# Two transformer layers on one core: a second transposed-x and shift tile, x in a ring of four, and new tables of jobs

## The reference

```python
xn = _layernorm(x)
x = x + _L0_attn_ref(xn, ...) + _L0_ffn_ref(xn, ...)   # differential attention: 2 x 16 maps of 4 features; FP6-quantised 128x128 product
xn = _layernorm(x)
x = x + _L1_attn_ref(xn, ...) + _L1_ffn_ref(xn, ...)   # rotary attention: 16 heads of 8 features; three products with +-1 weights
```

## Time and profile before

| | |
|---|---|
| median of 3 runs | 860.66 us |
| the profiled execution's own time | 859.55 us |
| its span, first to last instruction | 857.8 us |
| first exponential starts | 20.53 us |
| PE / ACT / DVE busy | 93% / 89% / 64% of the span |
| ACT's exponentials, 768 of them | 725.8 us busy |
| mean granted clock of TensorE | 0.989 |

### The profile page before, as it was taken

One profiled execution on the slowest core, in us unless ns is written; L12 is line 12 of the kernel. 1 busy time (PEld: TensorE's weight loads), 2 busy tenths in 40 slices (PEclk: granted clock), 3 DMA queues, 4 the chain that ended last, 5 costly groups with the idle time before them and its releaser, 6 DMA issues.

```text
span 857.8 us, 17781 instructions
## 1 busy us (share of the span) xinstructions
PE 801.4 (93%) x6735; PEld 283.6 (33%) x6735; DVE 551.5 (64%) x1216; ACT 764.2 (89%) x856; POOL 35.4 (4%) x56
## 2 busy tenths in 40 slices
...
GB/s 110 166 119 123 53 91 135 124 57 50 164 50 148 7 106 108 107 97 2 164 50 141 64 1 213 50 126 30 51 164 89 115 2 151 53 2 139 75 13 13
DMA packets 42114, 75.52 MB, mean 88 GB/s; under 512 B 5920, under 2 KB 7584, under 8 KB 42016
## 3 DMA queue, kind: packets, MB, share of 16 engines
...
...
## 4 chain that ended last, share of the span: by engine, by line
PE 70%; ACT 12%; DVE 9%; issue 5%; DMA 2%; SPq 1%; DVEq 0%; ACTq 0%
PE ps_pv L899 30%; PE ps_s L880 20%; ACT probs L726 12%; PE ps_misc L747 7%; PE ps_misc L751 7%; PE ps_misc L752 5%; PE ps_misc L740 2%; DMA q_ab<-shift 1%; DMA parts_dram<-qk_parts 1%; DVE pv_sb L1346 1%; DVE v_aug L1205 0%; DVE h_lo L1139 0%; ACT ff_out L676 0%; SPq L457 0%; DVE h_hi L1137 0%
## 5 line engine op out<-in xcount | busy, mean ns | idle before, releaser
L726 ACT ACTIVATE probs<-ps_s 128x1024 f32<-128x1024 f32 x768 | 725.8, 1048 | 54.8 <-PE ps_s L880 53.7
L899 PE MATMUL ps_pv<-probs,v_aug 128*32 128x512 f32 x3072 | 412.0, 608 | 8.6 <-ACT probs L726 4.6
L880 PE MATMUL ps_s<-q_ab,k_ab 18*128 18x512 f32 (+1 forms) x1088 | 142.6, 497 | 29.9 <-ACT probs L726 23.9
L880 PEld LDWEIGHTS ps_s<-q_ab,k_ab 18*128 18x128 f32 (+1 forms) x1088 | 54.6, 183 | 204.1 <-ACT probs L726 164.1
L899 PEld LDWEIGHTS ps_pv<-probs,v_aug 128*32 128x32 f32 x3072 | 61.7, 108 | 116.2 <-issue 82.8
L751 PE MATMUL ps_misc<-h_hi,k_w 128*128 128x512 f32 x192 | 85.8, 447 | 2.4 <-DVE v_aug L1205 1.2
L880 PE MATMUL ps_s<-q_c,k_c 34*128 34x512 f32 x448 | 84.1, 451 | 0.0
L1137 DVE CAST h_hi<-ff_out 128x512 fp32r<-128x512 f32 x64 | 27.4, 427 | 86.9 <-ACT ff_out L676 85.1
L1346 DVE STREAM_TRANSPOSE pv_sb<-ps_pv 128x512 f32<-128x512 f32 x48 | 34.4, 717 | 74.6 <-PE ps_pv L899 72.0
L752 PE MATMUL ps_misc<-h_lo,k_w 128*128 128x512 f32 x192 | 75.9, 395 | 0.0
L751 PEld LDWEIGHTS ps_misc<-h_hi,k_w 128*128 128x128 f32 x192 | 35.9, 187 | 88.9 <-issue 50.4
...
## 6 DMA issues: line engine op xcount, KB each, us to landing
...
q_ab<-parts_dram SPq DMA_DIRECT2D x60, 128.0 KB, 4.7
k_ab<-parts_dram SPq DMA_DIRECT2D x60, 128.0 KB, 6.0
...
```

What stands on the lines that cost most here:

```text
L726: nc.scalar.activation(probs[:, U.slot(s), 2 * half:2 * half + 2], ps_s[:, 2 * pair:2 * pair + 2], ACT.Exp, scale=SCALE[U.layer]).then_inc ...
L880: ins = nc.tensor.matmul(ps_s[:, bank, :], k[row:row + n, slot, c * P:(c + 1) * P], q[row:row + n, slot, :], start=True, stop=True)
L899: ins = nc.tensor.matmul(ps_pv[32 * j:32 * j + 32, :], v_aug[:, U.v, c, a:a + 32], probs[:, U.slot(s), j, :], start=c == 0 and not odd, st ...
```

## The change

- `xn_t` and `shift` become two tiles each, one per layer (`xn_ts`, `shifts`); DVE waits before the short branch of `exact` only for the shift loads of its own layer.
- `x_all` becomes `x_ring` with four places, sequence b in place b mod 4. POOL loads 1 to 3 at first, and b + 2 after `x_t1` of b, when the store of b - 2 has landed. The parked values of sequences 5 and 6 both use place 0, that of sequence 4: DVE waits for five landed stores before it parks them.
- 16 transposes of the identity (`WARM_AGAIN`) are put ahead of the first scores.
- The tables are new. In `FIRST`, `norm0`, `x_t0`, `q0`, `k0` and `exact0` of sequence 2 move from units B1 and C0 to B0 and A1; in A0 and B0 some jobs change steps. In `LOOP`, `v1` goes from step 9 of the A table to step 7, and `rope`, `q1`, `k1`, `ff2_b`, `combine` move a step or so. In `LAST`, `project1` of 4 goes from step 12 of A6 to step 7, ahead of `v1` of 5 in step 10.
- SP writes q and k of sequence 2 ahead of its load of B1, whose shift rows it loads first.

```diff
+RING = 4
...
+WARM_AGAIN = 16
...
-     9: [("regroup", 1, "A", 1), ("take", 1, "B", 0), ("q0", 2)], 10: [("regroup", 1, "B", 0)], 11: [("k0", 2)],
...
+    {1: [("norm0", 2, 4), ("regroup", 0, "B", 1)], 2: [("x_t0", 2), ("combine", 0, 0), ("combine", 0, 1)],
+     3: [("q0", 2), ("combine", 0, 2), ("combine", 0, 3), ("combine", 0, 4)], 4: [("k0", 2)], 5: [("combine", 0, 5)],
+     6: [("out_t0", 0)], 7: [("exact0", 2), ("project0", 0), ("norm1", 0, 0)], 8: [("norm1", 0, 1)],
...
+     5: [("exact1", 0), ("ff0", 0, 2)], 6: [("ff0", 0, 3)], 8: [("ff1", 0, 0)], 9: [("regroup", 1, "A", 1), ("take", 1, "B", 0)],
+     10: [("regroup", 1, "B", 0)], 11: [("ff1_b", 0, 0)], 13: [("quant", 2, 0), ("quant", 2, 1), ("quant", 2, 2)],
...
-     7: [("rope", -1, "k", 0), ("rope", -1, "k", 1)], 9: [("v1", -1), ("take", 0, "A", 0), ("qk_norm1", -1)], 10: [("ff0", -1, 3)],
...
+     7: [("rope", -1, "k", 0), ("rope", -1, "k", 1), ("v1", -1)], 9: [("take", 0, "A", 0), ("qk_norm1", -1)], 10: [("ff0", -1, 3)],
...
-     11: [("qk_norm1", 5)], 12: [("project1", 4)], 13: [("exact1", 5), ("ff1", 5, 0), ("ff1_b", 5, 0), ("norm0", 7, 0)],
...
+     5: [("k1", 5)], 7: [("rope", 5, "k", 0), ("project1", 4)], 8: [("rope", 5, "k", 1), ("take", 6, "A", 0)], 9: [("ff0", 5, 3)],
+     10: [("v1", 5)], 11: [("qk_norm1", 5)], 12: [("regroup", 6, "A", 0)],
...
-        x_all = sb("x_all", [P, NSEQ, T, D], F32)
+
+        x_ring = sb("x_ring", [P, RING, T, D], F32)
...
-        xn_t = sb("xn_t", [P, N], F32)
+        xn_ts = [sb(f"xn_t{layer}", [P, N], F32) for layer in range(2)]
...
-        shift = sb("shift", [2 * H, PARTS, N], F32R)
+        shifts = [sb(f"shift{layer}", [n, PARTS, N], F32R) for layer, n in enumerate(HEADS)]
...
+        def x_of(b):
+            return x_ring[:, b % RING]
...
+        waiting_values = x_ring[:, 4 % RING]
...
             scores_done(unit("A", 1))
+            load_shift(sp, unit("B", 1))
+            writes(0, 2)
             load_qk(unit("B", 1))
-            load_shift(sp, unit("B", 1))
             writes(1, 0)
             load_qk(unit("C", 0))
             load_shift(sp, unit("C", 0))
-            writes(0, 2)
...
-            for b in range(1, NSEQ):
-                if b == 2:
-                    pool.wait_ge(scores_made, 2 * STEPS)
-                pool.dma_start(x_all[:, b], x_dram[b].rearrange("p (t d) -> p t d", t=T)).then_inc(x_loaded if b > 1 else x1_loaded, 16)
+            def load_x(b, loaded):
+                pool.dma_start(x_of(b), x_dram[b].rearrange("p (t d) -> p t d", t=T)).then_inc(loaded, 16)
+
+
+            load_x(1, x1_loaded)
+            pool.wait_ge(scores_made, 2 * STEPS)
+            for b in range(2, RING):
+                load_x(b, x_loaded)
...
+            def load_next(b):
+
+                if RING <= b < NSEQ:
+                    pool.wait_ge(stored, 16 * (b - RING + 1))
+                    load_x(b, x_loaded)
...
+                        load_next(b + 2)
...
+                            warm(WARM_AGAIN)
...
-                    elif (layer, b) == (0, 2):
-                        dve.wait_ge(x_loaded, 16 * (NSEQ - 2))
+                    elif layer == 0 and b > 1:
+                        dve.wait_ge(x_loaded, 16 * (max(b, RING - 1) - 1))
...
-                    dve.wait_ge(stored, 16 * finished[0])
-                    taken(nc.vector.tensor_copy(x_all[:, b - 5].rearrange("p t d -> p (t d)"), ps))
+                    assert finished[0] == 5
+                    dve.wait_ge(stored, 16 * 5)
+                    wait(dve, v_moved, b - 5)
+                    taken(nc.vector.tensor_copy(waiting_values.rearrange("p t d -> p (t d)"), ps))
...
-                for stack, times in loads_due.items():
-                    wait(dve, shift_loaded[stack], times)
+                sh = [shifts[layer][:, i, :] for i in range(PARTS)]
+
+                for stack in "AB" if layer == 0 else "CDE":
+                    wait(dve, shift_loaded[stack], loads_due[stack])
```

More of the change, by code:

```diff
@@ L76 @@
     {0: [("v0", 0)], 1: [("fast", 0, "k", 1)], 3: [("setup", 0)], 5: [("quant", 0, 0), ("quant", 0, 1)],
-     6: [("quant", 0, 2), ("quant", 0, 3), ("quant", 0, 4)], 7: [("quant", 0, 5)], 9: [("take", 0, "A", 0)],
-     10: [("quant", 0, 6), ("quant_w", 0), ("norm0", 1, 0)], 11: [("w_t", 0), ("regroup", 0, "A", 0)],
-     12: [("norm0", 1, 1), ("bias", 0), ("quant_mm", 0)], 14: [("norm0", 1, 2), ("norm0", 1, 3)], 15: [("norm0", 1, 4), ("x_t0", 1)]},
-    {0: [("q0", 1)], 1: [("take", 0, "A", 1)], 2: [("lambda", 0), ("regroup", 0, "A", 1)], 3: [("quant", 1, 0)],
-     4: [("v0", 1), ("quant", 1, 1), ("quant", 1, 2)], 5: [("k0", 1)], 6: [("quant", 1, 3)], 7: [("quant", 1, 4)],
-     9: [("exact0", 1), ("take", 0, "B", 0)], 10: [("regroup", 0, "B", 0)], 11: [("quant", 1, 5), ("quant", 1, 6)],
-     12: [("bias", 1)], 13: [("quant_mm", 1)]},
@@ L84 @@
-    {1: [("take", 0, "B", 1), ("regroup", 0, "B", 1), ("combine", 0, 0)], 3: [("combine", 0, 1), ("combine", 0, 2)],
[7 rows of a table removed]
-     13: [("ff1", 0, 0), ("quant", 2, 0), ("quant", 2, 1), ("quant", 2, 2), ("quant", 2, 3), ("ff1_b", 0, 0)],
-     14: [("ff1", 0, 1), ("quant", 2, 4)], 15: [("quant", 2, 5), ("quant", 2, 6)]},
+     6: [("quant", 0, 2), ("quant", 0, 3), ("quant", 0, 4), ("quant", 0, 5)], 9: [("take", 0, "A", 0)],
+     10: [("quant", 0, 6), ("quant_w", 0), ("norm0", 1, 0)], 11: [("w_t", 0)], 12: [("norm0", 1, 1)],
@@ new lines @@
+     13: [("norm0", 1, 2), ("quant_mm", 0)], 14: [("norm0", 1, 3), ("bias", 0)],
+     15: [("norm0", 1, 4), ("x_t0", 1), ("regroup", 0, "A", 0), ("take", 0, "A", 1), ("regroup", 0, "A", 1)]},
+    {0: [("lambda", 0)], 1: [("q0", 1)], 3: [("quant", 1, 0)], 4: [("quant", 1, 1), ("quant", 1, 2)], 5: [("k0", 1)],
+     6: [("quant", 1, 3)], 7: [("quant", 1, 4), ("v0", 1)], 9: [("exact0", 1), ("take", 0, "B", 0)],
+     10: [("regroup", 0, "B", 0), ("quant", 1, 5)], 11: [("quant", 1, 6)], 12: [("bias", 1)],
+     13: [("quant_mm", 1), ("norm0", 2, 0), ("norm0", 2, 1)], 14: [("norm0", 2, 2), ("norm0", 2, 3)], 15: [("take", 0, "B", 1)]},
```

55 lines of the change are left out of this document (27 added, 28 removed), and 40 rows, old and new, of tables (FIRST, LAST, LOOP).

## The result

Eleven runs of the changed kernel have a median of 853.31 us (849.05 to 856.04), eleven of the kernel before on the same chip 860.95 (857.38 to 864.65). The ratio is 0.9912, with a 95% interval of 0.9892 to 0.9931: faster by 0.9%. The forecast was 849.0. The profiled execution takes 852.29 us against 859.55, so 7.3 us less where 10.6 were forecast. Its span is 850.5 us.

A forecast was written before the change was run, and what follows sets the result against it. It took PE (93% busy) and ACT (89%) as both near full, with steps of 1.83 us and about 0.47 us more per PE job. Its terms sum to -10.6 from the profiled 859.55 us: 849.0 us, range 845.0 to 855.0.

The forecast's parts named there:

- the likeliest case: Whole kernel: the forecast itself, all terms holding as priced; 849.0 us, chance 0.72.
- rival a: A1 is overfull: DVE's longer chain makes PE wait and lowers its clock; 852.7 us, chance 0.12.
- rival c: B1's relief comes back in C0 and A2; 855.8 us, about 857 with A0's gain lost; chance 0.04.
- Term 3: A1: sequence 2's work costs three PE jobs and waits for DVE; +3.3 us, bounds +1.4 and +5.
- Terms 1 and 2: Start: 16 transposes keep PE's clock up, -1.9 us; A0 and B0: new job places, -0.5 us.
- Term 2: A0 and B0: new places spare some waits, w_t still waits and the clock falls as before; -0.5 us.
- Term 4: B1: losing sequence 2's work frees DVE and leaves eight jobs; -5.8 us, bounds -3.5 and -6.3.
- Term 5: C0: exact0 of sequence 2 is gone from DVE ahead of combine 1's last part; -0.3 us.
- Term 6: A2 to A5: v1 away from qk_norm1 saves 1.3 us in each of four units; -5.2 us.
- term 7: LOOP's other moves (ff2_b, q0, combine's end) leave each job at 0.47 us; -0.2 us, bounds -1 and +1.
- Term 8: The ring: in A6 sequence 4's store lands before DVE parks v1 of sequence 5; 0 us, bounds 0 and +2.5.
- rival b: Clock falls at 20 us despite the transposes (+1.9), A6's store lands by its median (+1.8); 852.7 us, chance 0.09.

The follow-up runs named there:

- e7: The changed kernel with k of sequence 7 made in step 5 of B6, ahead of three quantization jobs, instead of step 7; 852.38 us, ratio 0.9908.
- e1: The changed kernel without the 16 transposes ahead of the first scores; 850.96 us, ratio 0.9885.
- e6: The changed kernel with the first five units' tables and SP's order as before the change (sequence 2's q and k in B1 again); 853.25 us, ratio 0.9921.
- e3: The changed kernel with identity transposes in two PE waits of A1, 7 before project0 and 14 before step 10's value product; 848.20 us, ratio 0.9851.
- e10: The changed kernel with B6's take moved to step 9, ahead of bias and the last quantization job; 854.63 us, ratio 0.9941.
- e12: The changed kernel with sequence 2's shift job late, k of sequence 7 early and B6's take ahead of bias and quantization; 846.95 us, ratio 0.9858.
- e4: The changed kernel with 20 transposes of the identity before w_t in step 11 of A0; 852.05 us, ratio 0.9874.
- e5: The kernel before the change with only v1 moved, from step 9 to step 7 of the loop's A table; 857.67 us, ratio 0.9962.
- e9: The changed kernel run again with no edit; 852.62 us, ratio 0.9933.
- e11: The changed kernel with e12's table edits and 20 transposes of the identity before w_t; 845.98 us, ratio 0.9851.

## Why the prediction was right in sign and off by four us

**The total.** Faster by over 0.5%, as forecast with 0.93, and 853.3 lies in the range. But the likeliest case did not hold; rival a did, which had 852.7 and a chance of 0.12. By the prediction's own test ("wrong if A1 is above 37") its account failed: A1 is above 37 in this profile, and in four of the five others with the same table. That the total still came within 4.3 us owes something to luck: 1.8 us of gains beyond the forecast, 1.1 of them in units for which it had no term, made up for part of A1. One sum has a slip: rival c's "about 857" is 857.7 by its own terms; nothing rests on it.

**Term 3 is the step that failed.** Priced at +3.3, measured +7.3, beyond its upper bound of +5, which had jobs and waits in it and no clock. Jobs and waits came to 4.5 (e7), within that bound. What they consist of, by steps of A1 in e7: k0 of sequence 2, +1.3, since PE waits 0.60 us until q0 leaves the shared bank; the first jobs of sequence 2, +0.7; project0, one step later, -0.9 and +2.1; the value product of step 10, +1.35, which waits 1.78 for the take. I had 1.4 for three jobs, 0.8 for project0 and 1.1 for the take, and not the wait of k0, whose bank DVE empties behind parts of combine: I added the new DVE instructions on the way to out_t0, but did not ask where the short PE jobs between them would wait for the bank. The views to have used are the totals: 7 us more of DVE work in a unit of 31.4 in which it had been busy 21.4, while the 6.08 us of idleness that I counted on lie at its beginning. The other 2.8 is the clock. I had seen that mechanism in B1 and put it for A1 into a rival of 0.12, where it came in five of six profiles.

**Terms 1 and 2.** The first is right in its place (7.35 to 5.44 us in steps 0 to 2, forecast -1.9). Against a kernel without the transposes it is 0.95 (e1), as the stretch can be 3.41 or 6.83 us long: one execution shows one draw. Term 2 had -0.5 and came out at +0.65 with the start and B0, because the fall at w_t, which I took to be the same as before, was twice as long. B0's 0.3 us repeat in every profile with full clock there. Whether the tables gain anything in A0 is not shown: with the transposes at the start and 3.41 us at half clock at w_t, the old tables take 34.52 (e6), the new ones 34.70, 34.70 and 34.44 (e3, e10, e12). The 33.6 without any fall (e4) has no counterpart with the old tables.

**Term 4** is right (-6.15 for -5.8): eight jobs at 0.47 gave 33.1 and the profile 33.17. Part of it is the clock that no longer falls in B1. The mean of 0.47 us a job held for these eight; my addition of 0.4 for ff1 was not needed. **Term 5** is right (-0.33 for -0.3).

**Term 6** is right in size (-5.5 for -5.2) and half wrong in its reason. "v1 away from qk_norm1" alone is worth 2.1 (e5), since the wait goes to step 7; the rest needs q1 and k1 a step earlier, which term 7 priced with other moves at -0.2. The comparison with A6 gave the right size; a likely reason, which no run tested, is that in A6 q1 and k1 stand early too (steps 2 and 5).

**Term 7** is right in sum (-0.35 for -0.2) and not in its reason that each job stays at 0.47: ff2_b cost 0.83 us in step 15 of B3 (2.65 to 1.82) and costs 0.72 in step 1 of C2 (1.81 to 2.53). The B units' -3.02 and the C units' +2.67 are mostly this job changing units.

**Term 8.** 0, as forecast, with a landing of 2.5 us and 2.3 us to spare before DVE parks the values. By the figures of the Trainium skill, "DMA: Bandwidth & Descriptors", section "Anatomy of one DMA — SWDGE (gpsimd) path", the estimate for 256 KB is 2.6 us. This store agrees with 2.5; the median of the seven stores here, 6.9, does not. The rival b needed the median, and both halves of it failed.

**Not foreseen**: B6 to C7 gave 1.1 us. 0.6 of it is the wait for A7's load (2.37 us before, 1.76 here), which lay between 1.45 and 2.71 in profiles in which B6's table is the same, so it is as likely a draw as a gain.

What stays open: what decides whether the clock falls, and for how long. The executions show falls in or close behind waits of 2.92 us (w_t), 1.19 to 1.97 us (A1), 2.35 to 2.71 us (A7's start), 1.11 us (B6 in e9) and even 0.64 us (A0 in e7) or 0.71 and 0.48 us (B0 in e11), but also a wait of 1.78 us in A1 (e7) and one of 1.76 us at A7's start (the changed kernel) with none behind them. No experiment varied one wait in small steps.
